# A graph network on one core: one window and ScalarE's one-hots per tile, duplicate sums and degrees moved into the attention loop, late scatters held to the weighted sum's pace

## The reference, cut to what matters

```python
# 0  relational: per edge the row h[src] @ weight_r[type]; mean over a node's edges
deg = segment_sum(ones, dst);  M = segment_sum((h W)[etype, src] / deg[dst], dst)
x  += relu(0.2 h + 0.8 M)                      # h = relu(layernorm(x)) in each layer
# 1  attention: e = tanh([h[src], h[dst]] @ W_attn.T + b) @ w_out, softmax over each dst
x  += segment_sum(alpha[:, None] * h[src], dst)
# 2  Chebyshev, K = 3: two products with the weighted, normalised adjacency
deg = segment_sum(edge_weight, src);  w = -dis[src] * edge_weight * dis[dst]
x  += (1 - Z) * H_tilde                        # Z, H_tilde from X, Tx1, Tx2
# 3  graph convolution: x += A (h W) + b, with A the weighted adjacency
```

## Time and profile before

| | before |
|---|---|
| span of the profiled execution | 2006.4 us |
| its own time | 2008.18 us |
| median of three runs | 2007.6 us |
| busy: PE / DVE / ACT / POOL | 1255.5 / 987.9 / 199.7 / 1257.9 us |
| busy share: PE / DVE / ACT / POOL | 63% / 49% / 10% / 63% |
| mean DMA rate | 136 GB/s |

### The profile page before, as it was taken

How to read it: one execution, slowest core, us unless ns; L and a number is a source line. 1 busy time by engine, 2 the same in 40 slices (tenths; PEclk the granted TensorE clock), 3 DMA queues, 4 the chain that set the end, 5 groups by cost and what they waited for, 6 DMA issues and landing times.

```text
span 2006.4 us, 28723 instructions
## 1 busy us (share of the span) xinstructions
PE 1255.5 (63%) x7844; PEld 1021.6 (51%) x7845; DVE 987.9 (49%) x2889; ACT 199.7 (10%) x390; POOL 1257.9 (63%) x1381
## 2 busy tenths in 40 slices
PE   5454555555563457767676664999865005599678
PEld 2354545455553456666676663999821001244323
DVE  8757565666566234344444445777540000102788
ACT  3000000000000021212111121111100000001100
POOL 0677677777778777777777777777786777000000
PEclk9778777777785655555555555999887557899799
DMA  6646455455520222222222230000236006689497
GB/s 185 206 140 187 149 161 167 149 167 170 176 56 3 58 70 78 79 77 79 76 80 79 76 80 20 1 0 0 111 151 262 0 0 262 215 347 409 173 415 310
DMA packets 154645, 272.07 MB, mean 136 GB/s; under 512 B 44030, under 2 KB 100154, under 8 KB 151546
## 3 DMA queue, kind: packets, MB, share of 16 engines
q1 hardware_dynamic: 111322, 229.57, 31.9%
q0 software_dynamic: 40064, 41.32, 8.9%
q10 hardware_dynamic: 3232, 0.82, 0.2%
HBM read 215.32 MB, written 56.29 MB: 135 GB/s over the span
## 4 chain that ended last, share of the span: by engine, by line
POOL 42%; issue 23%; PE 17%; DMA 10%; DVE 5%; ACT 1%; POOLq 1%; SPq 0%; ACTq 0%; DVEq 0%
POOL rings L735 23%; POOL pairs_by_src L752 18%; PE acc L986 7%; PE acc L1034 7%; DMA rings<-relation_rows,idx_ring 5%; DMA rings<-attention_rows,idx_ring 3%; DVE big L1825 2%; DMA pairs_by_src<-fed_val,fed_idx 1%; ACT big L900 1%; DMA big<-pairs_by_src 1%; POOL fed_val L743 1%; PE acc L992 0%; POOL fed_idx L744 0%; PE acc L1284 0%; PE acc L1224 0%
## 5 line engine op out<-in xcount | busy, mean ns | idle before, releaser
L986 PE MATMUL acc<-rings 128*65 128x128 f32 x3328 | 474.3, 307 | 256.5 <-DMA rings<-relation_rows,idx_ring 244.5
L986 PEld LDWEIGHTS acc<-rings 128*65 128x65 f32 x3328 | 414.6, 157 | 275.1 <-issue 262.5
L735 POOL DMA_INDIRECT rings<-relation_rows,idx_ring x416 | 412.7, 992 | 186.5 <-issue 124.4
L752 POOL DMA_INDIRECT pairs_by_src<-fed_val,fed_idx x416 | 423.3, 1017 | 132.6 <-issue 122.8
L1028 PE MATMUL acc<-attend_mem,rings 128*128 x1664 | 368.2, 423 | 183.5 <-DVE rings L1366 183.5
L735 POOL DMA_INDIRECT rings<-attention_rows,idx_ring x416 | 392.9, 945 | 132.2 <-issue 118.8
L1028 PEld LDWEIGHTS acc<-attend_mem,rings 128*128 128x128 f32 x1664 | 358.8, 332 | 193.1 <-issue 193.1
L1034 PE MATMUL acc<-big,attend_mem 128*64 128x512 f32 x700 | 175.3, 638 | 164.6 <-DMA big<-pairs_by_src 164.6
L1034 PEld LDWEIGHTS acc<-big,attend_mem 128*64 128x64 f32 x700 | 57.8, 146 | 260.8 <-DMA big<-pairs_by_src 175.0
L1424 DVE TENSOR_SCALAR rings<-iota_bf,col_local,score 128x256 f32<-128x256 bf16 x416 | 140.6, 409 | 44.5 <-PE acc L986 43.0
L1679 DVE TENSOR_TENSOR rings<-acc,rings 128x512 f32<-128x512 f32 x52 | 36.0, 692 | 248.7 <-DMA rings<-attention_rows,idx_ring 248.7
(11 more groups left out here) (279 smaller groups left out, 916.8 us busy)
## 6 DMA issues: line engine op xcount, KB each, us to landing
big<-pairs_by_src SPq DMA_DIRECT2D x54, 2048.0 KB, 13.5
pairs_by_src<-zeros SPq DMA_DIRECT2D x24, 1792.0 KB
big<-key_rows SPq DMA_DIRECT2D x52, 512.0 KB
rings<-local_rows SPq DMA_DIRECT2D x52, 256.0 KB, 3.3
big<-pairs_by_src SPq DMA_DIRECT2D x12, 1024.0 KB, 12.1
rings<-relation_rows,idx_ring POOLq DMA_INDIRECT x416
pairs_by_src<-fed_val,fed_idx POOLq DMA_INDIRECT x416
rings<-attention_rows,idx_ring POOLq DMA_INDIRECT x416, 2.5
```

Source lines behind the costliest of these rows:

```text
L735: pool.indirect_dma_start(ring[h][:, u, 0:width], None, table, bass.IndirectOffsetOnAxis(ap=idx_ring[h][:, u:u + 1], axis=0),).then_inc(ga ...
L752: pool.indirect_dma_start(pairs_by_src, bass.IndirectOffsetOnAxis(ap=fed_idx[:, h, u:u + 1], axis=0), fed_val[:, h, u:u + 1], None).then_i ...
L986: m = pe.matmul(node_sums[:, bass.ds(at[u] * P + w * P, P)], rows[h][:, u, :], onehot[h][:, u, w * P:(w + 1) * P], start=False, stop=False ...
```

## The change

- A tile's one-hot has 128 columns and begins at its first destination. The sums stand in eight PSUM banks of 512 columns that overlap by 128 (`sum_at` holds the column), so one matmul does for a tile in `add_up`; `turn_nodes` adds the overlaps.
- In the relation stage ACT makes the one-hots (`window_hots`: |column - position|, then relu(1 - that)). DVE only sums the duplicates of the first 64 tiles there (`early_dups`).
- Duplicates of the other tiles and the degrees are computed in the attention loop (`tile_hots`, `take_dups`, and two groups of matmuls in `look_up`). Duplicates are no longer sent to a dump area: each writes the same sum.
- `onehot_rows` is one instruction of 1024 columns; `look_up` has one matmul a tile that finds both candidates, of which `copy_predicated` takes one.
- The zeroes are written in halves, from the fifth pass on each after a gather half-step.
- Late scatters: after the first pass of 16, each of 14 passes waits until the weighted sum is four half-steps further.

```diff
+    PACE = 4
 def window_hots(it, h):                                   # ACT, new
+    act.wait_ge(rows_free["rel"], it * 4 + 2 * h + 2)
+    for u in range(H):
+        o = act.activation(onehot[h][:, u, :], iota_bf[:, 0:P], ACT.Abs, scale=-1.0,
+                           bias=col_window[:, bass.ds(it * (2 * H) + (h * H + u), 1)])
+    o.then_inc(away_ready, 1)
+    act.wait_ge(away_ready, it * 2 + h + 1)
+    act.activation(onehot[h], onehot[h], ACT.Relu, scale=-1.0, bias=1.0).then_inc(onehot_ready["rel"], 1)
 def add_up(key):                                          # PE
-            for w in range(2):
-                m = pe.matmul(node_sums[:, bass.ds(at[u] * P + w * P, P)], rows[h][:, u, :],
-                              onehot[h][:, u, w * P:(w + 1) * P], ...)
+            m = pe.matmul(node_sums[:, bass.ds(at[u], P)], rows[h][:, u, :], onehot[h][:, u, :], ...)
 def look_up(key):                                         # PE
-            for w in range(2):
-                m = pe.matmul(work[2 + h][:, u * D:(u + 1) * D], onehot_t[h][:, w, u * P:(u + 1) * P], ...)
+            m = pe.matmul(found[h][:, u * 2 * D:(u + 1) * 2 * D], onehot_t[h][:, u * P:(u + 1) * P], there, ...)
         m.then_inc(slot_free[key], 1)
+        pe.wait_ge(hots_ready, it * 2 + h + 2)
+        for u in range(H):
+            pe.matmul(degree_bank, onehot_lo[h][:, u, :], hi_parts[h][:, u, :], ...)
+        for u in range(H):
+            m = pe.matmul(dup_bank[h][:, u, :], eq[h][:, u, :], parts_ring[h][:, u, :], ...)
+        m.then_inc(degrees_added, 1)
 def early_dups():                                         # DVE, new; four passes
+        dve.tensor_tensor(early_eq[h], early_keys[h], col_key[:, cols]...to_broadcast([P, H, P]), ALU.is_equal)
+        dve.tensor_tensor(early_eq[h], early_eq[h], early_weights[h], ALU.mult).then_inc(early_read, 1)
+        dve.tensor_reduce(early_val[:, cols], early_eq[h], AX.X, ALU.add).then_inc(early_ready, 1)
 def onehot_rows(key, here, it, h):                        # DVE
-    for w in range(2):
-        for e in range(0, H * P, 2 * P):
-            o = dve.tensor_scalar(onehot_t[h][:, w, e:e + 2 * P], local_ring[h][:, e:e + 2 * P],
-                                  iota_part[:, w:w + 1], None, ALU.is_equal)
+    dve.tensor_scalar(onehot_t[h][:, :], local_ring[h][:, :], iota_part[:, 0:1], None, ALU.is_equal)
 def scatter_step(it, val, first, last, summed):           # POOL
         for h in range(2):
+            if h == 0 and summed is not None:
+                pool.wait_ge(slot_free["agg"], summed)
 def scatter(first, end, val, val_ready, at_first, at_last, pace=False):
+    paced = a + 1 + (2 * IT) // PACE if pace else a + 1
+    if pace:
+        with pool.Fori(a + 1, paced) as it:
+            scatter_step(it, val, summed=it * PACE + 2 - a * PACE)
+        scatter_step(paced, val, summed=FREED)
```

More of the change, by code:

```diff
@@ L56, in gnn_kernel @@
     VB = N // P
+    SPAN = BANK - P
+    TOP = VB * P
+    SUM_BANKS = 8
+    assert SUM_BANKS * SPAN == TOP and SPAN % P == 0 and NODES == TOP + P
+    PER_SPAN = SPAN // P
     SLOTS = 6
@@ L242, in gnn_kernel @@
         stat = [sb(f"stat{i}", [P, NB, 1]) for i in range(6)]
+        degree = sb("degree", [P, NB, 1])
         dis = sb("dis", [P, NB, 1])
@@ L902, in attention_step @@
                     act.wait_ge(bank_read, it * 2 + h + 3)
+                    if not last:
+                        act.activation(upper_ring[h][:, :], col_upper[:, bass.ds((it + 1) * (2 * H) + h * H, H)], ACT.Copy
+                                       ).then_inc(upper_ready, 1)
                     act.activation(msg[h][:, :, :], msg[h][:, :, :], ACT.Tanh).then_inc(tanh_ready, 1)
@@ L966, in clear_sums @@
                     pe.wait_ge(wait, 2)
-                for i in range(MAIN + 1):
+                for i in range(SUM_BANKS):
+                    if key == "agg" and i == SUM_BANKS - 1:
+                        pe.wait_ge(expo_ready, 1)
                     m = clear(banks[i])
-                    if i >= MAIN - 1:
+                    if key == "agg" and i >= SUM_BANKS - 2:
                         m.then_inc(slot_free[key], 1)
@@ L976, in add_up @@
                         _, at = nc.values_load_multi_w_load_instructions(
-                            block_at[0:1, bass.ds(it * (2 * H) + h * H, H)], engines=[PE_ENGINE], min_val=0, max_val=NB - 1,
-                            skip_runtime_bounds_check_because="a node's block, below NB")
+                            sum_at[0:1, bass.ds(it * (2 * H) + h * H, H)], engines=[PE_ENGINE], min_val=0,
+                            max_val=SUM_BANKS * BANK - P, skip_runtime_bounds_check_because="a window's column, within a bank")
                         pe.wait_ge(onehot_ready[key], it * 2 + h + 1)
@@ L1010, in turn_nodes @@
+                    if twice:
+                        t = pe.matmul(acc[:, c:c + D1], node_sums_t[0:D1, x - P:x], ident[0:D1, 0:D1],
+                                      start=False, stop=True, skip_group_check=True)
                 t.then_inc(nodes_turned, 1)
@@ L1014, in look_up @@
                 for h in range(2):
-                    pe.matmul(work[2 + h][:, :], zeros[:, 0:P], zeros[:, :], start=True, stop=True
-                              ).then_inc(slot_free[key], 1)
+                    for i in range(2):
+                        m = pe.matmul(found[h][:, i * BANK:(i + 1) * BANK], zeros[:, 0:P], zeros[:, :], start=True, stop=True)
+                    m.then_inc(slot_free[key], 1)
+                clear(product_bank)
+                clear(banks[3]).then_inc(degrees_added, 2)
                 with pe.Fori(0, IT) as it:
```

455 lines of the change are left out of this document (243 added, 212 removed).

## The result

The changed kernel takes 2037.9 us (median of four runs, 2033.25 to 2039.14), the kernel before 2007.3 in the same session: ratio 1.0157, 95% interval 1.0135 to 1.018. It is slower, by 30 us, where 2016 was forecast. The profiled execution is the 2033.25 one, with a span of 2031.4 us: 25.0 more than that of before.

The account below looks back on a forecast made before the run. POOL's issue of indirect DMA descriptors was taken to bound the kernel up to the last scatter. From the profiled 2008.2 us: +5 preparation, -24 + 6 relation stage, +3 attention, +18 wait gives 2016; range 2005 to 2044.

Parts of the forecast that it names:

- Preparation, +5: Before the first gather: DVE has more preparation work, so POOL's first gather starts 5 us later; bounds 3.5 and 6.5.
- Relation stage, -24 + 6: Relation gathers: shorter DMA instructions and pauses save 24 us; early duplicates on DVE cost POOL 6 us, bounds 0 and 19.5.
- The floor: Relation stage: its gathers can get as short as attention's, 525 us in place of 549; all 24 us taken.
- Early scatters, 0: 64 scatters beside layer 0's end: the edits there lie beside POOL's 93 us and change nothing.
- The new wait, +18: Late scatters: POOL stalls before its 17th until four half-steps of the weighted sum are done, losing 16 to 20 us.
- Attention, +3: Attention stage: DVE and PE stay behind POOL; 3 us for jitter and the broadcast of keys, bounds 0 and 35.
- a rival of its own: Attention: one 1024-column one-hot instruction stops POOL 0.59 us a half-step, 31 us in place of 3, total 2044; chance 0.20.
- Passes, 0: Passes after the last scatter: nothing in them is edited, so they only shift with it; 0 us.
- Gain and wait cancel: Whole kernel: early duplicates cost POOL nothing, wait at its low end, attention at 0, total 2005 us; chance 0.13.

Follow-up runs that it names:

- the edits from both sides: Last tile's padding lanes given their own addresses in the changed kernel: 2025.2 us; padding lanes put at one address in the kernel before: 2016.6 us.
- The three edits: Changed kernel without late-scatter waits, with padding lanes at own addresses and transposed one-hots in four pieces: 2470.6 and 2475.9 us on slower chips.
- the single gains: Changed kernel with one edit each: no late-scatter waits 2021.9 us, padding lanes at own addresses 2025.2, transposed one-hots in four pieces 2033.0.

## Why the prediction was right, and where its size was wrong

**Direction and range held**: slower was forecast at 0.73, 2037.9 lies inside 2005 to 2044. The likeliest value was 22 us low; the measured time lies outside the forecast's own range of 2008 to 2024. That the kernel is slower clear of noise is in part luck: without the two misses below (8.4 and 11.8 us) the parts that were forecast rightly add up to about 2013, 5 us over the kernel before, where the prediction takes 4 for noise.

**Preparation, +5**: +5.3. The first gather started at 60.1, still released by DVE's queue.

**Relation stage, -24 + 6**: -20.8. The floor was right: without the six slow gathers the stage would be 528.2 - 4.0 = 524.2 long, attention's length of before (524.8). The early duplicates cost 4.0 and not 6. The forecast had POOL pay for both instructions of each half-step; in the trace it paid for L1480 alone, in six of eight half-steps, each time because 0.25 us or more of it was still to run when a gather started. L1483 started 0.04 to 1.09 us into a gather, had at most 0.15 us left at the next one's start, and cost nothing. That DVE's short instructions were what lengthened the gathers before is the forecast's reading; the counts above bear it out, and it was not tested by itself.

**Early scatters, 0**: -0.5.

**The new wait, +18**: 19.5 us in the trace, 17.8 net in the stretch and 18.5 when taken away; released by PE at 1258.4, where 1262 to 1266 was worked out. Both its ends came earlier, mostly since the whole stage had moved (attention ended at 1217.1 for 1221.7): POOL was ready at 1239.7 (1259.20 - 19.53) in place of 1245.81.

**Attention, +3: the step that was mis-sized.** It measured 11.4. The sum had put 3 us for jitter and the keys and left the long instruction to a rival of its own, as all or nothing: "it would strike in nearly every half-step or in nearly none", 31 us or 0. The place of L1443 against the gathers drifts, and it struck in 28 of 52 half-steps, by 0.12 to 0.47 us each: 7.8 us, where neither the 0 nor the 31 was right. The 3 us put in for jitter and keys match the 3 us of longer pauses, which may be chance, since these vary by more than that from run to run. The premise that the stages are locked to POOL's rhythm holds only to a few tenths of a microsecond, and these decide. The step's other claim held: PE was busy 4.4 us of a half-step (229.03/52), 3.8 of them in the look-up, where 7 were taken for all of it, and no gather waited for DVE's `rows_free`.

**Passes, 0: the step that failed.** "Nothing in them is edited" was true of the code and not of what they wait for. The landing of the last scatter is part of that stretch, the change edits its addresses, and the last tile is nearly all padding. +11.0 of the +11.8 is this landing, and the edits from both sides show its cause. The description of the change says it ("each writes the same sum"); the step to ask how many lanes of a tile share a sum was left out.

With these two, 8 + 8.4 + 11.8 - 3 (the relation stage's surplus gain and small rests) is the 25 us between the spans. **Gain and wait cancel** was the right picture of the rest: preparation, relation stage and wait add to +2.3.

## What to carry to other kernels

When duplicates are let through to a scatter instead of being sent to a dump area, count the lanes that share an address, the padding of the last tile first; the price is small (11 us here), but it falls on the very landing that others wait for. A halved instruction count on engines off the path is worth only what it takes off the engine that bounds: 21 us in the relation stage, where the gathers got shorter, and less than nothing in attention, where one long instruction made of many short ones held the gathers up. An interlock that holds one engine to another's pace should be measured on more than one chip: on chip 5 it costs 18 us and gives nothing, on the slower ones the engines that it would serve stand still without it, and what it does there is open.

## What the hardware did that had not been expected

A scatter of 128 lanes of which 123 write one cell landed 18.05 to 18.38 us after its start, in four traces, and 7.09 and 7.37 us with cells of their own. That fits writes done one behind the other at an estimated 0.09 us each, but only this one number of lanes was measured. The Trainium skill (DMA: Bandwidth & Descriptors, § Rules for kernel authors) says that each duplicate's write goes out on its own, and that one lands; it gives no time for it.

POOL pauses at fixed places: ahead of the 113th, 225th and 337th DMA of each of its three long series, 141 to 165 us apart, in all six traces at 2007-us speed. The pauses are 1.7 to 2.2 us long at their shortest, also beside a DMA share of 0.42 (1.95 to 1.97 in the relation stage after the change), and up to 6.0 in the late scatters where loads run. The first of the late ones was 4.74 to 5.38 us in the three runs with the wait, whose loads of the first regions have begun by then (at 1367 in the changed kernel), and 1.69 to 1.70 in the three without it. So the wait brings some 3 us more by this way, of which 2 are left in the 17.8 us of the late stretch. What the pauses are is open.

Chips differ by 26% on the same kernel (2007 us on one, 2536 to 2539 on two others), and what a change is worth differs with them. The three edits are 2.5% faster than the kernel before on the slower ones. On the faster one the single gains add up to 2038 - 16 - 12.7 - 4.9 = 2004, which would be level with the 2007 of the kernel before; that is an estimate from three runs, since the three together have no run there.
